# GpSimd's small operations moved between the twelve steps of an image in a vision tower

## The reference

```
h   = wavelet(x)                      # Haar analysis, gates, Haar synthesis, per image
h   = h + attention(layernorm(h))     # 16 heads of 16 columns, causal, S = 256 rows, E = 256
h   = h + experts(layernorm(h))       # router, top 32 rows of each of 16 experts, two products, silu, a third product
layernorm(x) = (x - mean) / sqrt(var + 1e-5)
attention: q, k, v = x W + b;  scores = q k^T + causal mask;  out = softmax(scores / 4) v
```

## Time and profile before

| | |
|---|---|
| time, median of 3 runs | 1171.4 us (1171.28 to 1172.09) |
| the profiled execution's own time | 1171.56 us |
| its span | 1169.8 us |
| busy in the span | PE 85%, DVE 56%, ACT 50%, POOL 63% |

### The profile page before, as it was taken

How to read it: one execution, slowest core, us unless ns; L and a number is a source line. 1 busy time by engine, 2 the same in 40 slices (tenths; PEclk the granted TensorE clock), 3 DMA queues, 4 the chain that set the end, 5 groups by cost and what they waited for, 6 DMA issues and landing times.

```text
span 1169.8 us, 19244 instructions
## 1 busy us (share of the span) xinstructions
PE 992.1 (85%) x6998; PEld 826.0 (71%) x6998; DVE 655.2 (56%) x1502; ACT 590.3 (50%) x1105; POOL 732.5 (63%) x658
## 2 busy tenths in 40 slices
PE   0534986989889899886379999999999999999996
PEld 0213465777777777664258888888888888888885
DVE  5866664777777777653733453453453443453441
ACT  0112224777777877785334454454454454454442
POOL 4455434887888888796235665666576575665654
PEclk9778897999999999886679999999999999999999
DMA  8223789778877877601315455445455445455333
GB/s 214 72 72 108 144 188 131 111 140 145 142 142 138 139 145 131 98 30 46 108 55 104 113 104 109 113 86 109 113 104 108 113 86 109 114 104 107 78 55 37
DMA packets 105951, 127.62 MB, mean 109 GB/s; under 512 B 12288, under 2 KB 92160, under 8 KB 104832
## 3 DMA queue, kind: packets, MB, share of 16 engines
q1 hardware_dynamic: 81280, 92.81, 36.4%
q0 software_dynamic: 24576, 33.57, 17.7%
HBM read 79.67 MB, written 46.14 MB: 108 GB/s over the span
## 4 chain that ended last, share of the span: by engine, by line
PE 49%; DVE 2%; POOL 1%; issue 1%; DMA 0%; ACT 0%; POOLq 0%; ACTq 0%
PE y_ps L1172 16%; PE gate_ps L1158 15%; PE value_ps L1158 15%; PE xT_ps L1139 2%; DVE top_index L1312 1%; DVE top L1306 1%; DVE work L1314 0%; PE gate_ps L1181 0%; POOL out L1114 0%; POOL x_rows L1103 0%; DMA x_rows<-normed_scratch,slot_row 0%; DMA rw2s<-in_L_ffn_router_w 0%; ACT xg_hi L1205 0%; DVE L L1304 0%; DVE rw_shifted L1296 0%
## 5 line engine op out<-in xcount | busy, mean ns | idle before, releaser
L1114 POOL DMA_INDIRECT out<-y_rows,slot_row x128 | 202.9, 1585 | 192.2 <-ACT y_rows L1218 163.0
L249 POOL TENSOR_TENSOR probs_k<-probs_full,probs_k 128x512 f16<-128x512 f32 x192 | 223.1, 1170 | 66.9 <-ACT probs_k L650 66.6
L1281 DVE TENSOR_TENSOR hidden<-silu_g,value_ps 128x512 f32<-128x512 f32 x128 | 88.1, 688 | 306.2 <-PE value_ps L1158 171.4
L1226 ACT ACTIVATE silu_g<-gate_ps 128x512 f32<-128x512 f32 x128 | 76.6, 598 | 276.6 <-PE gate_ps L1158 276.6
L1103 POOL DMA_INDIRECT x_rows<-normed_scratch,slot_row x128 | 146.9, 1148 | 56.3 <-issue 38.7
L643 ACT ACTIVATE probs_full<-scoresT_ps,log 128x512 f32<-128x512 f32 x192 | 131.8, 687 | 87.3 <-PE scoresT_ps L474 55.8
L1172 PE MATMUL y_ps<-w_hi,hidden_lo 128*128 128x256 f32 x512 | 144.9, 283 | 0.0
L1172 PE MATMUL y_ps<-w_lo,hidden_hi 128*128 128x256 f32 x512 | 144.9, 283 | 0.0
L1172 PE MATMUL y_ps<-w_hi,hidden_hi 128*128 128x256 f32 x512 | 144.7, 283 | 0.0
L650 ACT ACTIVATE probs_k<-probs_full 128x512 f16<-128x512 f32 x192 | 119.7, 624 | 0.0
L1158 PE MATMUL gate_ps<-xg_hi,w_hi 128*128 128x512 f32 x256 | 103.4, 404 | 2.1 <-ACT xg_hi L1205 2.1
(11 more groups left out here) (206 smaller groups left out, 2333.3 us busy)
## 6 DMA issues: line engine op xcount, KB each, us to landing
w_raw<-in_L_ffn_w SPq DMA_DIRECT2D x48, 512.0 KB, 4.1
q_stack<-q_scratch SPq DMA_DIRECT2D x96, 128.0 KB, 4.8
k_stack<-k_scratch SPq DMA_DIRECT2D x96, 128.0 KB, 7.6
x_tile<-in_x SPq DMA_DIRECT2D x4, 1024.0 KB, 5.0
h_scratch<-rec_tile SPq DMA_DIRECT2D x4, 1024.0 KB, 3.9
hacc<-h_scratch SPq DMA_DIRECT2D x4, 1024.0 KB, 5.4
q_scratch<-q_hi SPq DMA_DIRECT2D x16, 256.0 KB, 2.2
q_scratch<-q_lo SPq DMA_DIRECT2D x16, 256.0 KB, 2.5
```

Of the source, the lines that this page charges most:

```text
L249: G.tensor_tensor(probs(b, 1, n), pf[N % 3][:].rearrange("p (a q) -> p a q", a=4 if n % 3 == 2 else 2), probs(b, 0, n), ALU.subtract).then ...
L1114: G.indirect_dma_start(out=rows, out_offset=bass.IndirectOffsetOnAxis(ap=idx[:, col:col + 1], axis=0), in_=ys[c][:, j, :], in_offset=None, ...
L1226: A.activation(sg[ft % 2][:], GP[ft % 2][:], ACT.Silu).then_inc(silu_done, 1)
L1281: V.tensor_tensor(hf[ft % 2][:], sg[ft % 2][:], VP[ft % 2][:], ALU.mult).then_inc(hf_done, 1)
```

## The change

The first layer norm starts six steps earlier (`LN1` -36, and `FIRST` with it); `CUT` is now written as (-18, -6), the same steps as before. On POOL the two `rstd` come ahead of `probs_lo` within a step. `v_rest` moves from phase 4 to phase 6, `v_done` from 7 to 10, ACT's `v_mid` (line 716) from 6 to 8, the first norm's `rstd` from 8 to 2; the second norm's stays in phase 8. On DVE the second norm's refinement and normalising are one step later each. One wait is new, at step 19 on POOL.

```diff
-    LN1, XT, QP, KP, VP_, EX, MT, LN2, HT, RT = -30, -21, -18, -16, -12, 22, 13, 42, 53, 58
+    LN1, XT, QP, KP, VP_, EX, MT, LN2, HT, RT = -36, -21, -18, -16, -12, 22, 13, 42, 53, 58
     FIRST, LAST = LN1, 12 * (B - 1) + RT + 1
-    CUT = (FIRST + 12, FIRST + 24)
+    CUT = (-18, -6)
...
@@ POOL, ticks
+                    if t == 19:
+                        g.wait_ge(v_rest, 3)
                     if 15 <= t < 20:
                         clear(3, t - 15)
+                    b, r = due(t, LN1 + 2)
+                    if r == 0:
+                        rstd(0, b)
+                    b, r = due(t, LN2 + 2)
+                    if r == 0:
+                        rstd(1, b)
                     b, r = due(t, EX + 1)
                     if b >= 0:
                         probs_lo(b, r)
-                    b, r = due(t, LN1 + 2)
-                    if r == 0:
-                        rstd(0, b)
-                    b, r = due(t, LN2 + 2)
-                    if r == 0:
-                        rstd(1, b)
-                    b, r = due(t, VP_ + 4)
+                    b, r = due(t, VP_ + 6)
                     if r == 0:
                         g.wait_ge(v_hi, b + 1)
...
-                    if r == 3:
+                    if r == 4:
                         g.wait_ge(v_mid, b + 1)
...
@@ ACT, ticks
-                    if r == 3:
+                    if r == 5:
                         act.wait_ge(v_rest, b + 1)
...
@@ DVE, ticks, second norm
-                    if r == 3:
+                    if r == 4:
                         ln_first(1, b)
-                    if r == 4:
+                    if r == 5:
                         ln_second(1, b)
-                    if r == 5:
+                    if r == 6:
                         ln_rstd(1, b)
```

More of the change, by code:

```diff
@@ L271, in ticks @@
                             g.wait_ge(rec_out[x], 32)
+                    if t == 19:
+                        g.wait_ge(v_rest, 3)
                     if 15 <= t < 20:
                         clear(3, t - 15)
-                    b, r = due(t, EX + 1)
-                    if b >= 0:
-                        probs_lo(b, r)
                     b, r = due(t, LN1 + 2)
@@ L282, in ticks @@
                         rstd(1, b)
-                    b, r = due(t, VP_ + 4)
+                    b, r = due(t, EX + 1)
+                    if b >= 0:
+                        probs_lo(b, r)
+                    b, r = due(t, VP_ + 6)
                     if r == 0:
```

## The result

The changed kernel takes 1161.1 us, the median of four runs (1160.8 to 1164.3), beside 1171.6 for the kernel before in the same comparison: a ratio of 0.992, with an interval of 0.991 to 0.994. On a second chip the ratio is 0.9945 (0.9927 to 0.9962). The profiled execution took 1161.27 us with a span of 1159.4. The forecast was 1153.5 in a range of 1147 to 1163: the direction is right, and of the 18.1 us forecast 10.3 came in the profiled execution.

A forecast was written before the change was run, and what follows sets the result against it. The prediction took PE's expert stage, run as a block after `front`, and before it a closed loop of waits among engines as the bound. Start 3.9 + steady state 11.7 + tail 2.5 = 18.1 us off 1171.56: 1153.5, range 1147 to 1163.

The forecast's parts named there:

- POOL's order in the steady state: Ten images of the attention stage: a shorter POOL burst removes PE's waits at line 449, 11.7 us (8 to 15).
- the stand for the power: DVE's wait for POOL's power in the second norm, 26.1 us in all, 2.4 each: all of it goes.
- PE's wait at the scores: PE's wait on DVE's row maximum at line 449, phase 0: its 11.7 us nearly vanish.
- The rival of the held-up normalising: Phase 0: POOL's low halves hold up DVE's second-norm pair, up to 0.85 us an image; 1157.5 to 1162, chance 0.18.
- two of the signs that the prediction named: Forecast wrong if normalising takes far over 0.8 us a pair, or PE's idle time turns up at another line.
- The forecast distance: Steady state: line 293's operations, POOL's additions to `hacc`, come about 21.8 us apart, from 22.94 an image.
- the bound behind it: Steady state: a microsecond off POOL's burst is worth about one off the image, from one image of 21.89 us.
- "Nothing" for V's moves and for the second norm a step later: Steady state: moving `v_rest`, `v_mid`, `v_done` and the second norm's DVE work later costs nothing.
- the cover that I named: DVE's V sum follows `v_done` by four phases, 7.6 us, against 1.16 of work, so the moves cost nothing.
- The start: Before the first images: earlier `xT_lo` of image 1 brings DVE's last wavelet tile and PE's synthesis 3.9 us forward (0 to 4.5).
- The tail: After 455 us: two more PE waits of the same kind, 3.1 us together, go; 2.5 us taken (0 to 3.1).
- The rival that ends slower: POOL's `rstd` ahead of `probs_lo` delays low halves in some 28 places; mean stand 0.65 us decides, 1.3 gives 1190; chance 0.06.

The follow-up runs named there:

- number 1: The changed kernel with DVE normalising the first norm in phase 10 instead of phase 7: 1158.2 us, ratio 0.9898 to the kernel before.
- number 2: The kernel before with only the early first norm (the `LN1` and `CUT` lines of the diff): 1158.1 us, ratio 0.9898.
- number 4: The kernel before with only V's three moved operations and the new wait at step 19: 1172.1 us, ratio 1.0029.

## Why the prediction came out as it did

- *POOL's order in the steady state: 11.7 forecast, 2.9 measured.* The waits went as forecast: the stand for the power, and PE's wait at the scores. The step that failed is "I count exactly those 11.7 us": it took a wait of PE that goes for time gained. The rival of the held-up normalising came true, in another place and at another price, with two of the signs that the prediction named: a pair far over 0.8 us, and PE's idle time at another line. I looked for it in phase 0, where the pair takes 1.12 us with no wait of PE for a row maximum behind it; it stands in phase 7, where the early norm put it and where POOL now runs the moved `v_rest`. And I priced it by a pair of 1.58 us, of which only the second operation, from 490.40 to 491.65, was held up by one of POOL's (490.27 to 491.50). The price is 2.44 - 0.75 = 1.7 us, of which 0.84 reached the distance (number 1). The whole price stood in the trace of the kernel before: in the wavelet stage two neighbouring operations of DVE each last about as long as one of POOL's tile 3, while the same lines take 0.28 and 0.35 us where POOL is idle. DVE, then POOL beside the first two; POOL's operation at 96.70 is in the earlier trace rows:

```profile
96.92 1.92 DVE L898 TENSOR_SCALAR v_scaled<-band,gate 128x128 f32<-128x128 f32 x1
98.87 2.00 DVE L900 SCALAR_TENSOR_TENSOR col_sum_dif<-band,gate,v_scaled 128x128 f32<-128x128 f32 x1
...
133.86 0.28 DVE L898 TENSOR_SCALAR v_scaled<-band,gate 128x128 f32<-128x128 f32 x1
134.18 0.35 DVE L900 SCALAR_TENSOR_TENSOR col_sum_dif<-band,gate,v_scaled 128x128 f32<-128x128 f32 x1
```
```profile
98.83 1.89 POOL L217 TENSOR_TENSOR col_dif_a<-x_tile 128x1024 f32<-128x1024 f32 x1
```

Nor are the 2.9 us POOL's order alone: with the early norm and the old order the ten images take 5.1 less (number 2), so that the rest of the change takes 2.2 of them back. The forecast distance was right once the pair was out of the way, 21.87 in number 1 where 21.8 was forecast. That does not show the bound behind it, a microsecond off the image for one off the burst: the burst ahead of the power lost more than two, the image one, and what holds the distance near 21.9 stays open.
- *"Nothing" for V's moves and for the second norm a step later.* Wrong for V's moves: alone they cost 0.40 us an image (number 4), although no wait on V arose, because the cover that I named was for what waits on these operations, not for what runs beside them. No run has the second norm's step by itself. In the kernel before, the pairs took 0.75 and 0.72 us in the middle because POOL, its burst just done, had gaps of 0.21 and 0.94 there. DVE, then POOL:

```profile
307.41 0.75 DVE L820 TENSOR_SCALAR hn<-hacc,mean_var,rstd 128x256 f32<-128x256 f32 x2
...
309.55 0.72 DVE L820 TENSOR_SCALAR hn<-hacc,mean_var,rstd 128x256 f32<-128x256 f32 x2
```
```profile
307.89 1.28 POOL L249 TENSOR_TENSOR probs_k<-probs_full,probs_k 128x512 f16<-128x512 f32 x1 [0.21 <-ACT probs_k L650]
310.12 1.16 POOL L249 TENSOR_TENSOR probs_k<-probs_full,probs_k 128x512 f16<-128x512 f32 x1 [0.94 <-ACT probs_k L650]
```

- *The start: 3.9 forecast, 3.2 measured* (A, 56.57 to 53.34). Right: `xT_lo` of image 1 at 115.18 (114.1 forecast), the synthesis at 133.38 (132), and a wait of 0.73 for `xT_hi` for which the sum has no term. The transposes of image 0 in the kernel before, and the three steps in the changed one:

```profile
79.20 1.09 PE L562 MATMUL mix_a_ps<-ident,hn 128*128 128x128 f32 x4 [19.02 <-DVE hn L820]
```
```profile
80.04 1.08 PE L564 MATMUL mix_a_ps<-ident,hn 128*128 128x128 f32 x4 [19.03 <-DVE hn L822]
...
133.38 1.12 PE L527 MATMUL scoresT_ps<-low,ident 128*128 128x512 f32 x2 [2.22 <-DVE low L912]
```
```profile
115.18 0.69 DVE L928 TENSOR_TENSOR xT_lo<-mix_a_ps,xT_hi 128x512 fp32r<-128x512 f32 x1 [0.73 <-ACT xT_hi L697]
```

The other 3.3 of the profile's 6.5 us have no term in the prediction: B gives 1.7, the transfer wait 2.2 and what follows it 0.7; the later transposes of image 0 take 0.8 back, and the way from those of image 2 to the transfer wait 0.4. B and the transfer wait have other values in other profiles with either `LN1`, and no run ties them to the change.
- *The tail: 2.5 forecast, 0.3 measured.* From the eleventh addition to the last it is 89.56 us before and 89.23 after; PE's waits for the row maxima there fell only from 3.1 to 2.0. The other 0.6 of the 0.9 us lies in the expert stage, which the change doesn't touch.
- *The rival that ends slower* met its condition, POOL at line 242 waiting for DVE's aggregation, but at 0.4 us in nine places, 3.6 in all, far from the 18 that decide.

The parts make 3.2 + 2.9 + 0.3 = 6.4 us, beside 10.3 between the two first profiles and 0.0055 x 1170 = 6.4 (4.4 to 8.5) on the second chip. Of the 3.9 us that the parts leave open on the first chip, 3.3 are the start's terms above. So it is in part luck that the time lies inside the stated range: the parts alone give 1171.56 - 6.4 = 1165.2, and so does the ratio of the second chip, which is outside it.

## What to carry to other kernels

When work is moved on GpSimd, list what VectorE runs beside its new place, not only who waits for its result: a normalising or a similar elementwise operation from memory to memory waits out each GpSimd operation that it meets, whatever its own size. Such operations belong into a phase where GpSimd has gaps or VectorE has slack, and the two are placed together: here POOL's moves alone brought nothing or a loss, and the pair's move alone a loss. Each part of a change is worth a run of its own: the early norm alone gave a ratio of 0.9898, all of the change together 0.9922 and 0.9945. A start that waits on transfers is compared by its steps and not by one profile: in two profiles of the kernel before, the first addition comes at 225.99 and at 222.21 us.

## What the hardware showed

- A pair of VectorE operations on 8 columns took 2.27 us beside back-to-back GpSimd operations, and one on 256 columns 2.44; alone the latter takes 0.73. The held-up time counts as busy and not as idle time in the profile: from 278 to 322 us VectorE is busy 37.24 us in the changed kernel and 33.38 before. The reductions, statistics and the operations that read PSUM between them kept their durations (`row_max` 0.65 to 0.69). The Trainium skill, "SBUF — State Buffer", § Who interferes with whom, says that GpSimd and VectorE in one of its two-port modes, which it lets `tensor_scalar` enter, exclude each other: the engine that issues first has the shared port pair for its whole instruction, and the other blocks fully. The trace agrees, with 2.27 us for 8 columns. That the second of two operations waits anew, for GpSimd's next one, is what the runs add. One that begins late in an operation of GpSimd waits only for the rest: in the kernel before, the first of a pair takes 0.42 us at 307.41, where GpSimd's operation ends at 307.69.
- After PE's stand of 2.2 us ahead of the last wavelet tile, the windows of 130 to 140 us have a granted clock of 1.00 (all at 2.4 GHz) in some profiles and 0.83 (partly at 1.2) in others. Its price is 1.65 us: the six products of `band` behind the first two take 4.39 us (at 136.78 in the kernel before) instead of 2.74 (at 134.34 in the changed one), and B is 19.2 instead of 17.5. What decides it stays open; both values occur with `LN1` at -30 and at -36.
